# The order of the first instructions in a two-layer graph attention kernel: values' weights and projections moved ahead, second unit and layer 1's weights reordered

## The reference

```python
h = jnp.maximum(_layernorm(x, axis=-1), 0.0)
x = x + gnn(h, Wq, bq, Wk, bk, Wv, bv, Wf, bf, adj)

def gnn(h, ...):
    q, k, v = heads(h @ Wq + bq), heads(h @ Wk + bk), heads(h @ Wv + bv)   # 6 heads of 64
    scores = einsum('bhqd,bhkd->bhqk', q, k) / sqrt(64)
    probs = softmax(scores + where(mask, 0, -9e15))
    return merge(einsum('bhqk,bhkd->bhqd', probs, v)) @ Wf + bf
```

## Time and profile before

| | us |
|---|---|
| median of three runs | 1851.24 |
| lowest and highest | 1850.74, 1851.70 |
| the profiled execution, its own time | 1853.11 |
| its span in the trace | 1851.3 |
| TensorE busy | 1821.8 (98%) |
| VectorE busy | 1621.9 (88%) |
| ScalarE busy | 1561.2 (84%) |
| GpSimd busy | 1490.9 (81%) |

### The profile page before, as it was taken

How to read it: one execution, slowest core, us unless ns; L and a number is a source line. 1 busy time by engine, 2 the same in 40 slices (tenths; PEclk the granted TensorE clock), 3 DMA queues, 4 the chain that set the end, 5 groups by cost and what they waited for, 6 DMA issues and landing times.

```text
span 1851.3 us, 54324 instructions
## 1 busy us (share of the span) xinstructions
PE 1821.8 (98%) x17210; PEld 1050.4 (57%) x17210; DVE 1621.9 (88%) x5551; ACT 1561.2 (84%) x4793; POOL 1490.9 (81%) x1781
## 2 busy tenths in 40 slices
PE   7899999999999999999999999999999999999998
PEld 3455555555555555555555555555555555555555
DVE  7889898898988988889888888988889888898876
ACT  5888888888888888888888888888888888888884
POOL 4678888888888888888888888888888888888761
PEclk8999999999999999999999999999999999999999
DMA  6656666666666666666667666667666666666655
GB/s 195 175 171 185 204 205 193 197 205 199 208 197 199 200 193 209 205 197 194 193 207 203 203 196 200 201 199 215 195 196 194 198 207 197 200 179 193 194 169 180
DMA packets 439942, 363.32 MB, mean 196 GB/s; under 512 B 207700, under 2 KB 406888, under 8 KB 439656
## 3 DMA queue, kind: packets, MB, share of 16 engines
q1 hardware_dynamic: 439656, 359.86, 65.1%
HBM read 184.30 MB, written 175.37 MB: 194 GB/s over the span
## 4 chain that ended last, share of the span: by engine, by line
PE 86%; DVE 4%; DMA 3%; SPq 3%; issue 2%; ACT 1%; POOL 1%; DVEq 0%; ACTq 0%; POOLq 0%
PE ps_qk L683 12%; PE ps_shared L683 12%; PE ps_shared L685 12%; PE ps_shared L684 12%; PE ps_qk L684 12%; PE ps_qk L685 12%; PE ps_shared L780 7%; PE ps_scores L800 7%; SPq L375 2%; DMA p_dram<-p_blocks 1%; DVE probs L1316 1%; DMA p_moved<-p_dram 1%; DVE qk_lo L1296 1%; POOL probs L551 1%; ACT probs L1013 1%
## 5 line engine op out<-in xcount | busy, mean ns | idle before, releaser
L1013 ACT ACTIVATE probs<-probs,row_min 128x128 f32<-128x128 f32 x1512 | 583.1, 391 | 2.5 <-DVE row_rcp L1281 1.5
L551 POOL TENSOR_TENSOR probs<-probs,row_rcp 128x768 f32<-128x768 f32 x252 | 370.2, 1469 | 215.5 <-DVE row_rcp L1281 215.2
L1316 DVE CUSTOM_DVE_ANT_0 probs<-ps_scores,mask,minus_scale 128x128 f32<-128x128 f32 x1512 | 429.6, 347 | 0.9 <-issue 0.6
L568 POOL TENSOR_TENSOR p_half<-p_moved,p_half 128x768 f16<-128x768 f32 x236 | 388.0, 1644 | 1.6 <-ACT p_half L988 1.6
L1296 DVE SCALAR_TENSOR_TENSOR qk_lo<-ps_qk,qk_bias,qk_hi 128x512 f16<-128x512 f32 x384 | 278.7, 747 | 77.2 <-ACT qk_hi L996 76.1
L1013 ACT ACTIVATION_READ_ACCUMULATOR probs<-probs,row_min 128x1 f32 x1512 | 288.8, 191 | 0.0
L996 ACT ACTIVATE qk_hi<-ps_qk,qk_bias 128x512 f16<-128x512 f32 x384 | 258.1, 672 | 14.6 <-PE ps_qk L685 14.6
L547 POOL TENSOR_TENSOR x_tile<-x_tile,out_bias 128x384 f32<-128x384 f32 x256 | 257.7, 1007 | 1.1 <-DVE out_bias L1240 1.1
L1327 DVE SCALAR_TENSOR_TENSOR x_tile<-ps_shared,out_scale,x_tile 128x384 f32<-128x384 f32 x256 | 157.1, 613 | 111.2 <-PE ps_shared L685 108.6
L683 PE MATMUL ps_shared<-wf_hi,ct_hi 128*128 128x384 f16 x768 | 250.6, 326 | 2.4 <-DVE ct_lo L1290 2.4
L685 PE MATMUL ps_shared<-wf_hi,ct_lo 128*128 128x384 f16 x768 | 250.8, 327 | 0.0
(11 more groups left out here) (152 smaller groups left out, 3997.7 us busy)
## 6 DMA issues: line engine op xcount, KB each, us to landing
p_dram<-p_blocks SPq DMA_DIRECT2D x256, 384.0 KB, 2.4
p_moved<-p_dram SPq DMA_DIRECT2D x1008, 96.0 KB, 2.4
h_dram<-h_blocks SPq DMA_DIRECT2D x252, 192.0 KB, 2.6
h_moved<-h_dram SPq DMA_DIRECT2D x1008, 48.0 KB, 2.0
x_tile<-in_x SPq DMA_DIRECT2D x128, 192.0 KB, 2.9
out_x<-x_tile SPq DMA_DIRECT2D x128, 192.0 KB, 2.7
adj_u<-in_adj SPq DMA_DIRECT2D x64, 64.0 KB, 2.6
p_half<-p_dram SPq DMA_DIRECT2D x16, 96.0 KB, 2.3
```

The lines of the kernel that those rows point to most:

```text
L551: nc.gpsimd.tensor_tensor(probs_of(t, i), probs_of(t, i), row_rcp[i % 2][:, :].rearrange("p (a o) -> p a o", o=1) .to_broadcast([P, HEADS, ...
L568: nc.gpsimd.tensor_tensor(p_part(i, 1), p_moved[i % 2][:, :, :].rearrange("p a n -> p (a n)"), p_part(i, 0), ALU.subtract).then_inc(p_set, 1)
L1013: ins = nc.scalar.activation(tile[:, s, :], tile[:, s, :], ACT.Exp, bias=row_min[i % 2][:, s:s + 1], scale=-1.0, accum_out=row_sum[i % 2][ ...
L1316: ins = nc.vector.tensor_tensor_reduce(tile[:, s, :], score_bank(i, s // PAIRS)[:, (s % PAIRS) * P:(s % PAIRS + 1) * P], mask[b][:, i, :], ...
```

## The change

Six orders are edited; no operation is added, removed or altered.

- **PE, unit 0:** three `project_v` come ahead of `turn_largest(0)`, the fourth ahead of `share_largest(0)`. In the second unit six pieces go ahead of `turn_largest(1)`, three more ahead of `share_largest(1)`, three more ahead of `sum_out_bias(1)`.
- **ACT, start:** values' high weight comes ahead of `h_hi(0, 0)`; `v_out(0, 0)` to `v_out(0, 2)` come ahead of other steps, the output's high weight after `relu(1, 2)`, the mask after `relu(1, 3)`.
- **DVE, start and second unit:** many steps are exchanged. `statistics(1, 2)` goes behind `find_other_scales(0)`, `spread_v_bias(0)` ahead of `find_peaks(0)`, `find_largest(1, 2)` and its neighbours behind `qk_lo_out(1, 0)`, `find_other_scales(1)` to nearly last.
- **ACT and POOL, slots 1 and 2:** layer 1's four weights are made at `i` = 0 and 2 of slots 1 and 2, before at every `i` of slot 1.
- The order of SP's DMAs stays.

```diff
@@ -584,8 +584,8 @@
                         p_lo(lu, li)
                     if exists(hu):
                         h_lo(hu, hi)
-                    if t == 1:
-                        next_weights_lo(CAST_ORDER[i])
+                    if t in (1, 2) and i % 2 == 0:
+                        next_weights_lo(CAST_ORDER[2 * (t - 1) + i // 2])
 
             def last_units():
                 add_out_bias(B, 0)
@@ -893,12 +893,12 @@
             keep_busy(2)
             turn_first(2)
             turn_first(3)
-            turn_largest(0)
             project_v(0, 0)
             project_v(0, 1)
+            project_v(0, 2)
+            turn_largest(0)
+            project_v(0, 3)
             share_largest(0)
-            project_v(0, 2)
-            project_v(0, 3)
             sum_out_bias(0)
             for piece in range(12):
                 project_qk(0, piece)
@@ -914,16 +914,15 @@
             score(0, 2)
             score(0, 3)
             turn_biases(1)
-            project_qk(1, 6)
-            project_qk(1, 7)
+            for piece in range(6, 12):
+                project_qk(1, piece)
             turn_largest(1)
-            project_qk(1, 8)
+            for piece in range(12, 15):
+                project_qk(1, piece)
             share_largest(1)
-            for piece in range(9, 12):
+            for piece in range(15, 18):
                 project_qk(1, piece)
             sum_out_bias(1)
-            for piece in range(12, 18):
-                project_qk(1, piece)
             project_v(1, 3)
             over_slots(slot)
             last_units()
@@ -1030,8 +1029,8 @@
                     hu, hi = graph_at(t, i, 8)
                     if exists(pu):
                         exp(pu, pi)
-                    if t == 1:
-                        weights_hi(1, CAST_ORDER[i])
+                    if t in (1, 2) and i % 2 == 0:
+                        weights_hi(1, CAST_ORDER[2 * (t - 1) + i // 2])
                     for cu, ci in pair_at(t, i):
                         if exists(cu):
                             ctx_hi(cu, ci)
@@ -1089,25 +1088,25 @@
 
             relu(0, 0)
             relu(0, 1)
+            weights_hi(0, 2)
             h_hi(0, 0)
+            relu(0, 2)
             h_hi(0, 1)
-            relu(0, 2)
-            weights_hi(0, 2)
             relu(0, 3)
             h_hi(0, 2)
             h_hi(0, 3)
+            v_out(0, 0)
+            v_out(0, 1)
             relu(1, 0)
             relu(1, 1)
-            v_out(0, 0)
-            v_out(0, 1)
-            relu(1, 2)
+            v_out(0, 2)
             weights_hi(0, 0)
             weights_hi(0, 1)
+            relu(1, 2)
             weights_hi(0, 3)
-            v_out(0, 2)
+            relu(1, 3)
             make_mask(0)
             h_hi(1, 0)
-            relu(1, 3)
             for chunk in range(3):
                 qk_hi_out(0, chunk)
             relu(2, 0)
@@ -1430,33 +1429,33 @@
             statistics(0, 1)
             find_value_peak()
             statistics(0, 2)
+            find_value_scale()
             statistics(0, 3)
-            find_value_scale()
             take_biases(0)
+            find_largest(0, 0)
+            weights_lo(2)
             first_lo(0)
-            find_largest(0, 0)
+            first_lo(1)
             find_largest(0, 1)
-            first_lo(1)
-            weights_lo(2)
+            first_lo(2)
+            find_largest(0, 3)
             find_largest_bias(0)
-            find_largest(0, 3)
+            first_lo(3)
+            spread_v_bias(0)
             statistics(1, 0)
-            first_lo(2)
-            first_lo(3)
+            find_peaks(0)
             statistics(1, 1)
-            find_peaks(0)
-            statistics(1, 2)
-            h_turn(1, 0)
             take_largest(0)
             find_scales(0)
+            h_turn(1, 0)
+            find_other_scales(0)
+            statistics(1, 2)
+            weights_lo(0)
             h_turn(1, 1)
-            find_other_scales(0)
-            spread_v_bias(0)
-            weights_lo(0)
+            statistics(1, 3)
+            weights_lo(1)
             h_turn(1, 2)
-            statistics(1, 3)
             statistics(2, 0)
-            weights_lo(1)
             statistics(2, 1)
             qk_lo_out(0, 0)
             h_turn(1, 3)
@@ -1468,7 +1467,6 @@
             h_turn(2, 0)
             h_turn(2, 1)
             find_largest(1, 3)
-            find_largest(1, 2)
             qk_lo_out(0, 4)
             qk_lo_out(0, 5)
             statistics(2, 2)
@@ -1476,34 +1474,35 @@
             mask_and_min(0, 0)
             mask_and_min(0, 1)
             h_turn(2, 2)
-            find_largest(1, 0)
-            find_largest(1, 1)
             qk_lo_out(1, 0)
             qk_lo_out(1, 1)
+            find_largest(1, 2)
+            find_largest(1, 0)
             take_biases(1)
             h_turn(2, 3)
+            qk_lo_out(1, 2)
+            find_largest(1, 1)
             find_largest_bias(1)
+            invert_sums(0, 0)
             spread_v_bias(1)
-            invert_sums(0, 0)
+            probs_turn(0, 0)
+            qk_lo_out(1, 3)
             find_peaks(1)
+            invert_sums(0, 1)
             take_largest(1)
-            probs_turn(0, 0)
             find_scales(1)
-            invert_sums(0, 1)
             statistics(3, 0)
-            qk_lo_out(1, 2)
-            qk_lo_out(1, 3)
             mask_and_min(0, 2)
+            probs_turn(0, 1)
+            qk_lo_out(1, 4)
             statistics(3, 1)
+            h_turn(3, 0)
+            qk_lo_out(1, 5)
+            keep_out_bias(1)
+            mask_and_min(0, 3)
             statistics(3, 2)
-            probs_turn(0, 1)
-            h_turn(3, 0)
-            mask_and_min(0, 3)
-            qk_lo_out(1, 4)
-            qk_lo_out(1, 5)
             find_other_scales(1)
             invert_sums(0, 2)
-            keep_out_bias(1)
             over_slots(slot)
             last_units()
 
```

## The result

The changed kernel takes 1854.24 us (median), the kernel before beside it 1850.51: 3.7 us more. The ratio is 1.0023, 95% interval 1.0016 to 1.0030, so it is slower by about 0.2%, and the interval lies clear of 1. One of the 15 executions took 2364.0 us at a granted clock of 0.75 and is not in the ratio; without it the median is 1854.0. Ratios and differences of medians don't agree to better than about 1.5 us in what follows, so both are given. The forecast was 1851.7 within 1847.6 to 1855.0: the time lies in the range, the direction is right, the size was taken too small, by 2.5 us against the stated 1851.7 and by 3.2 as a difference to the kernel before.

What follows compares the result with a forecast made beforehand. The prediction took PE, busy 98% of the span, as the bound. Second unit +2.9, first slot -2.7, clock +0.3 and second slot zero gave +0.5 on 1851.24, so 1851.7 us, range 1847.6 to 1855.0.

Steps and rivals of the forecast that it cites:

- Bound, and what is at stake: Whole kernel: PE binds; only its losses before about 101 us, some 18 us of waits and 3 of half clock, can change.
- Start, to the scales: Unit 0's start: value projections begin 3 us earlier, yet `take_largest(0)` comes at 21.7 against 21.77; 0.05 gained.
- Query weights: Before `project_qk(0, 0)`: PE waits 1.9 us and starts it at 26.6 instead of 28.22, 1.6 us ahead.
- What eats this: Unit 0's chain to `qk_lo_out(0, 0)`: it starts at 32.6 against 31.19; the 1.6 us lead and 1.3 more are lost.
- First scores: Before `score(0, 0)`: values' maximum no longer stands ahead, 1.0 us earlier, net 44.4 against 44.06.
- Second unit: DVE from `qk_lo_out(0, 0)`: `invert_sums(0, 2)` at 72.8 against 69.97, so `project_qk(2, 0)` at 75.5, 2.9 us later.
- 1.3 later: Lower end of the forecast delay of `project_qk(2, 0)`, whose likeliest delay was 2.9 us.
- First slot: Slot 1: odd steps lose their weights on ACT, PE's waits shrink, gain 2.7 us; 0.3 added for half clock.
- Second slot: Slot 2: ACT and POOL take the moved weights and both still fit; zero cost, 2.4 us if `ctx_hi` is late twice.
- rival (d): Slot 2: the moved weights bring two waits for `ct_lo` back, +2.4 us, 1854.2 us; chance 0.10.
- the prediction's own signs of being wrong: Wrong if `invert_sums(0, 2)` comes before 70, PE's clock stays low through several steps, or slot 2 exceeds 29 us.
- Sum: All terms: 2.9 - 2.7 + 0.3 = +0.5 us, ends -1.7 and +3.6, giving 1851.7 us.

Runs made afterwards that it cites:

- e7: Kernel before with layer 1's weights spread over slots 1 and 2, ScalarE's high weights behind `ctx_hi`; ratio 1.0000 to the kernel before.
- e8: Changed kernel with `statistics(1, 2)`, `h_turn(1, 1)`, `invert_sums(0, 2)` earlier, `find_scales(1)` ahead of `invert_sums(0, 1)`, high weights behind `ctx_hi`; ratio 1.0000 to the kernel before.
- e2: Kernel before with only unit 0's orders changed on TensorE, ScalarE and VectorE; ratio 1.0022 to the kernel before, +2.8 us by medians.
- e11: Changed kernel with only the spreading of layer 1's weights undone; ratio 1.0031 to the kernel before, +5.7 us by medians.
- e4: Changed kernel with `statistics(1, 2)` back behind `statistics(1, 1)` and `h_turn(1, 1)` ahead of the queries' low weights; ratio 1.0013 to the kernel before.
- e6: Changed kernel with `take_largest(1)` and `find_scales(1)` ahead of `invert_sums(0, 1)`; ratio 1.0015 to the kernel before, +3.5 us by medians.

## Why the prediction was right, and where its sizes were off

- **Bound, and what is at stake:** right in place. The kernels differ by their orders before 135 us; from 136 to 1830 PE waits 3.5 us in all in the changed kernel, 3.2 of it in the hand-written end. But in the kernel before it waits 6.7 there, 3.4 of it for `qk_lo`, and with the same code in that part e7 has 0.3 of that kind. So this scatter is as large as what was forecast, and the prediction gave it no term.
- **Start, to the scales:** right to half a microsecond. `project_v(0, 0)` at 14.4 (13.8), `turn_largest(0)` at 20.0 (19.7), `take_largest(0)` at 22.1 (21.7). The queries' maximum started at 11.16, when its weight had landed, not at 10.65, which is most of it; with the same order it starts at 9.89 in e8.
- **Query weights:** 1.1 us ahead and 2.05 of idle time (1.6 and 1.9 forecast).
- **What eats this:** right in mechanism. The term mis-sized is `qk_lo_out(0, 0)`: 34.0, not 32.6. Half a microsecond is the start's, the rest is the DMA queue. I gave `bring_h(1, 0)` the 1.86 us of the earlier trace rows, it took 3.47, and ACT waited 0.94 us for it. Both parts belong to this execution as much as to the order: the five profiles with this unit 0 have 31.95 to 34.01, and the distance from `take_largest(0)`, 10.9 us in the prediction, is 11.0 and 11.1 in e2 and e11, where ACT doesn't wait. POOL's stall was as taken: 1.19 us for a step of 0.19. The Trainium skill's page "SBUF — State Buffer" (section "Who interferes with whom") has such pairs exclude each other, and these rows agree with it. e4 shortens the chain and brings `qk_lo_out(0, 0)` forward, without telling its links apart; the mask and `h_hi(1, 0)`, which the prediction priced at 1.1 us and the rows at 1.3, remain in it.
- **First scores:** the forecast gain of 1.0 us is there (11.8 us from `qk_lo_out(0, 0)` to `score(0, 0)` in place of 12.9); the late start outweighs it.
- **Second unit:** `invert_sums(0, 2)` at 75.3 (72.8), so 41.3 us behind `qk_lo_out(0, 0)` where I had 40.2: right within 1.1. The stall of `find_scales(1)` was taken at 1.0 and is 1.4 by the two long rows, the second of them beside POOL's `h_lo`, which the prediction didn't have. The rest of the 1.1 was not followed. `project_qk(2, 0)` at 77.9 is 5.3 us late, not 2.9; 1.4 of the difference comes from the step above, 1.1 from here. (The lower end, "1.3 later", is 1.1 by the prediction's own terms: 31.9 + 33.7 + 5.5 + 2.67 against 72.64.)
- **First slot:** from `project_qk(2, 0)` to slot 2 it takes 27.1 us for 28.9: 1.8 gained, 2.4 forecast (2.7 less 0.3 for the clock). The clock stayed low longer: 9 of the matmuls of 512 columns from 77.94 on are 0.43 us apart, 4 before. Five more at 0.21 us each cost 1.1 us, not 0.3, so ACT's part was 2.9, near the 2.7.
- **Second slot:** forecast zero, with 2.4 as rival (d). It costs 1.4: the rival's mechanism at about half its price, as PE waits 0.42 and 0.64 us for `ct_lo` behind the weights that ACT makes (the other 0.3 us isn't put down to a wait). A second slot of over 29 us was one of the prediction's own signs of being wrong, and it took 30.1. This is the step whose likeliest value was wrong in kind: the room on ACT over the slot (22.60 of 28.78) said nothing about the place of the weights in the step, ahead of what PE waits for. e7 shows that the place makes it.
- **Sum:** 5.3 - 1.8 + 1.4 = +4.9 at slot 3, where +0.5 was forecast. In the medians it is 3.7. What makes up the other 1.2 us isn't known; the waits of the middle part differ from execution to execution by more than that.
- **Luck in the number:** +4.9 lies outside the sum's own ends (-1.7 to +3.6). With all of it in the median the time would be 1850.51 + 4.9 = 1855.4, past the stated 1855.0; it lies inside the range only because 1.2 us, of unknown cause, didn't arrive. The mechanisms hold; the measured time agrees better than the steps do.

## What to carry to other kernels

A step taken forward on one engine is gained only as far as the next shared resource lets it through: here PE's projections went forward 2.5 us and the third chunk still came late, since ScalarE now had the mask and another graph's high part ahead of the output that frees the bank, and a transpose through DRAM and a small statistics step, moved back as harmless, stood behind it. When two steps change place in an order, follow the one that goes back to its last consumer, and ask which instruction of another engine it will now run beside. Room in the sum of a stage is no room in a step: put additional work behind what the bounding engine waits for, not ahead of it.

## What the runs showed of the hardware

- A GpSimd step of 0.19 us takes 1.19 when it starts beside a VectorE instruction of 1.4 us with two inputs in SBUF, and VectorE's steps on three and two elements in each partition take 0.99 us beside GpSimd's 1.47 us scaling and 0.76 beside its 0.91 us `h_lo`, each until that instruction ends, and 0.17 and 0.15 when nothing runs beside them (e6). The pair stalls both ways.
- Four DMA issues took 1.86 us when they began at 24.96 (e4) and 2.57 to 3.47 when the same four began between 26.7 and 27.9 (the table above). One issue makes up the difference: in the changed kernel the first of the four takes 2.05 us, the others 0.43. The write ahead of them, issued at 27.46, lands 3.4 us later, the one at 23.91 1.9 us later. The kernel before has the same at the same time: its write at 27.04 lands 4.1 us later, that of 23.57 1.9, and one of the issues behind it takes 1.35. So the stretch from about 27 us on is slow for DMAs in either order, and the change moved a transfer that others wait for into it. What makes it slow wasn't tried.
- The queries' weight lands at times that differ by over 1 us between executions with the same order up to there (the maximum that waits for it starts at 9.89 in e8, 11.16 in the changed kernel), and how long TensorE's first matmuls stay at half speed differs as well (9 of them before, 17 in e7).
- After 2.05 us of idle time ending at 27.09 the granted clock is 0.50 from 28 to 30 us, the lower of the two levels (1.2 GHz), though TensorE is at work from 27.09 on, and 1.00 again from 31 us. By the rows it cost nothing here, since TensorE then idled 2.00 us for `qk_lo_out(0, 0)`; no run has it otherwise.
